# Routing logits from raw rows, a first expert pair selected by products, and filled waits on TensorE, in a two-layer graph and expert network

## The reference

```python
xn = layernorm(x)
x = x + graph_attention(xn, edges) + linear_attention(xn)      # layer 0
x = x + ffn0(layernorm(x))
#   mixed = xn @ wqkv.T ; q, k, v = split(mixed)               # 8 experts
#   logits[e] = sum_j softmax_j(q[e] * k[j]) * v[j]
#   top-2 of logits; scores = softmax(top-2)
#   out = sum over the two experts of score * (silu(a) * g) @ w2[e].T
xn = layernorm(x)
x = x + gat(xn, edges) + (layernorm(linear_attention(xn) @ W_fc + xn) * gamma + beta)
feats = layernorm(x)                                           # layer 1
x = x + ffn1(feats)
#   aff = feats @ centroids.T ; eid = argmax(aff)              # top-1 of 8
#   xhat = layernorm(feats)
#   y = feats + relu((xhat * gamma[e] + beta[e]) @ w1[e] + b1[e]) @ w2[e] + b2[e]
#   out = alpha * y + (1 - alpha) * feats, alpha = sigmoid(aff[eid])
```

## Time and profile before

| | us |
|---|---|
| median of the runs (3) | 1070.32 |
| lowest, highest | 1067.17, 1071.71 |
| the profiled execution | 1067.81 |
| its span, first to last instruction | 1065.9 |

### The profile page before, as it was taken

How to read it: one execution, slowest core, us unless ns; L and a number is a source line. 1 busy time by engine, 2 the same in 40 slices (tenths; PEclk the granted TensorE clock), 3 DMA queues, 4 the chain that set the end, 5 groups by cost and what they waited for, 6 DMA issues and landing times.

```text
span 1065.9 us, 9957 instructions
## 1 busy us (share of the span) xinstructions
PE 1006.1 (94%) x3388; PEld 542.7 (51%) x3388; DVE 362.1 (34%) x1008; ACT 201.7 (19%) x415; POOL 319.5 (30%) x247
## 2 busy tenths in 40 slices
PE   6999999999999999999958999989999999994997
PEld 4555555555555435544445566544444555453332
DVE  6044372156000147701233100171120265576214
ACT  3132321111111038800011111121110020012220
POOL 2888887888888800000000000010000000001210
PEclk9999999999999999999978999999999999995999
DMA  9655545544544630022166898663433115553997
GB/s 334 173 99 145 143 106 140 138 100 90 145 102 99 202 123 2 1 79 79 64 212 197 301 347 325 242 244 100 158 101 110 44 59 208 207 178 121 404 362 258
DMA packets 63852, 174.32 MB, mean 164 GB/s; under 512 B 22224, under 2 KB 22960, under 8 KB 63680
## 3 DMA queue, kind: packets, MB, share of 16 engines
q1 hardware_dynamic: 38800, 146.56, 40.3%
q0 software_dynamic: 20960, 15.63, 8.1%
q10 hardware_dynamic: 4048, 11.59, 3.0%
HBM read 161.79 MB, written 11.95 MB: 163 GB/s over the span
## 4 chain that ended last, share of the span: by engine, by line
PE 46%; POOL 24%; DMA 12%; issue 10%; DVE 6%; ACT 2%; SPq 0%; ACTq 0%; DVEq 0%; POOLq 0%
PE bank L1024 12%; PE bank L1000 10%; POOL n_lo L536 7%; POOL n_hi L536 7%; PE bank L1220 6%; POOL w_lo L536 5%; POOL w_hi L536 4%; PE bank L1013 4%; DMA G<-in_stream 3%; PE bank L1245 2%; PE bank L1112 2%; DMA Y<-in_stream 2%; PE bank L1374 1%; DMA n_hi<-count,ridx 1%; DMA Y<-xs,idx 1%
## 5 line engine op out<-in xcount | busy, mean ns | idle before, releaser
L1013 PE MATMUL bank<-xnT,ring 128*128 128x384 f32 x896 | 291.8, 486 | 1.8 <-ACT xnT L693 1.2
L1013 PEld LDWEIGHTS bank<-xnT,ring 128*128 128x128 f32 x896 | 170.1, 190 | 120.4 <-ACT xnT L693 1.5
L590 POOL DMA_INDIRECT Y<-xs,idx x10 | 10.5, 1046 | 527.6 <-DVE idx L1806 443.4
L536 POOL DMA_INDIRECT n_lo<-count,ridx x48 | 83.2, 1734 | 15.0 <-issue 14.1
L536 POOL DMA_INDIRECT n_hi<-count,ridx x48 | 80.2, 1672 | 16.4 <-issue 14.0
L1024 PE MATMUL bank<-ring,Y 128*128 128x512 f32 x192 | 83.6, 594 | 0.0
L1024 PE MATMUL bank<-ring,xnT 128*128 128x512 f32 x192 | 82.7, 592 | 0.0
L1013 PE MATMUL bank<-Y,ring 128*128 x256 | 82.7, 486 | 0.0
L1220 PE MATMUL bank<-ring,Y 128*128 128x352 f32 x256 | 78.7, 466 | 0.7 <-issue 0.7
L717 ACT ACTIVATE Y<-bank,sbias,scale 128x384 f32 (+1 forms) x48 | 32.2, 671 | 202.3 <-PE bank L1013 184.4
L1000 PE MATMUL bank<-ring,Y 128*128 128x512 f32 x160 | 70.0, 593 | 0.0
(11 more groups left out here) (305 smaller groups left out, 1073.2 us busy)
## 6 DMA issues: line engine op xcount, KB each, us to landing
ring<-in_stream SPq DMA_DIRECT2D x144, 512.0 KB
ring<-in_up SPq DMA_DIRECT2D x32, 704.0 KB, 5.9
Y<-in_stream SPq DMA_DIRECT2D x18, 512.0 KB, 6.6
G<-in_stream SPq DMA_DIRECT2D x16, 512.0 KB, 7.2
ring<-in_dn SPq DMA_DIRECT2D x7, 1024.0 KB, 5.8
rows<-keys SPq DMA_DIRECT2D x10, 512.0 KB
ys<-Y ACTq DMA_DIRECT2D x9, 512.0 KB, 7.6
xnT<-in_stream SPq DMA_DIRECT2D x6, 512.0 KB
```

Of the source, the lines that this page charges most:

```text
L536: pool.indirect_dma_start(table, bass.IndirectOffsetOnAxis(ap=at[:, e:e + 1], axis=0), what[:, e:e + 1], None, **how).then_inc(done, 16)
L590: pool.indirect_dma_start(dst, None, src, bass.IndirectOffsetOnAxis(ap=idx[:, col:col + 1], axis=0))\
L1013: last = pe.matmul(bank[to][:, 0:N], ring[:, r, k * P:(k + 1) * P], rhs(k), start=(k == 0), stop=(k == KB - 1))
```

## The change

1. Attention: `scores(1)` to `scores(4)` stand one behind each of the last four value chunks; `turn` waits for the bank that it writes instead of for all; VectorE weighs unit 2 ahead of reading unit 4.
2. First routing: TensorE transposes halves of the raw rows `xr` as soon as they are in the residual (`turn_raw`). The logits are those of raw rows; VectorE subtracts mean times the column sums of `wqkv` (a product with ones, `gate_sums`) and scales by `rstd` (`route_logits`). Blocks 0 and 1 are routed together, ahead of block 2's addition, block 2 alone. ScalarE takes two exponentials (`GL`, `GM`), with the square root of block 2 between them.
3. Second routing: the residual is written in halves; affinities come from raw rows (`turn_features`, `affinities`), corrected by the mean but not scaled, and the first maximum is taken ahead of the second normalisation. The features `xn` of the last block are written after the routing.
4. The first pair's rows are not gathered: a 0/1 mask `first_pair` is multiplied with the rows `xh` in SBUF (`select_first_pair`), which gives them already transposed. GpSimd gathers pairs 1 to 3 (`pairs`).
5. `keep_busy(n, to)` issues n products of 128x384 f16 into a bank that is not read: 1 + 26 behind the last logits, 3 + 7 in `list_rows`, 4 ahead of and 4 behind the first expert's turn, 6, 10 and 8 in the second routing.
6. `up` and `up_pair` wait for the two halves of the transposed rows apart.

The core of the diff, PE first, then ACT, DVE, POOL and SP:

```diff
+            def keep_busy(n, to):
+                for _ in range(n):
+                    pe.matmul(bank[to][:, 0:N], id16, iota, start=True, stop=True)
...
                 if kk == 0:
                     pe.wait_ge(v2_done, 2)
-                    scores(1)
-                elif kk >= 2:
-                    scores(kk)
-            scores(4)
-            pe.wait_ge(v2_done, 6)
+                scores(kk + 1)
...
+            def turn_raw(half, b):
+
+                pe.wait_ge(x1_done, half * NB + b + 1)
+                pe.wait_ge(t_evicted, T_LN2 + 2 * b + half - 1)
+                for k in range(4):
+                    last = pe.transpose(bank[half][:, k * P:(k + 1) * P],
+                                        xr[:, b, (4 * half + k) * P:(4 * half + k + 1) * P], ident)
+                last.then_inc(tp_ready, 1)
...
+            for b in range(1, NB):
+                block_rows(b, range(0, 2), tok(2), arrived, True, False)
+                for half in range(2):
+                    turn_raw(half, b - 1)
+                if b == 1:
+                    pe.matmul(bank[5][:, 24:48], ones, small_sums, start=True, stop=True).then_inc(pe_output, 1)
+                block_rows(b, range(2, 4), tok(2), arrived, False, False)
+                for half in range(2):
+                    raw_logits(b - 1, half)
                 block_rows(b, gnn_slots, tok(4), arrived, False, True)
-                if b:
-                    if b == 1:
-                        pe.wait_ge(x1_done, NB)
-                    logits(T_LN2, wqkv, 3 * NE, b - 1)
-            turn_block(T_LN2, NB, NB - 1)
-            logits(T_LN2, wqkv, 3 * NE, NB - 1)
+            turn_raw(0, NB - 1)
+            turn_raw(1, NB - 1)
+            raw_logits(NB - 1, 0)
+            keep_busy(1, 6)
+            raw_logits(NB - 1, 1)
+            keep_busy(26, 6)
...
+                keep_busy(3, spare)
                 for e in range(turns):
+                    if e:
+                        keep_busy(1, spare)
...
             rank_rows(R0)
-            list_rows(R0, NE, lambda b, e: slot[:, b, e, :])
+            list_rows(R0, NE, lambda b, e: slot[:, b, e, :], 6)
+            keep_busy(4, 6)
...
                 turn_rows(S, 0, True)
+                keep_busy(4, 6)
                 pe.wait_ge(R.rows_known, 2)
                 up_(0, 0)
...
+            def select_first_pair(half):
+
+                for k in range(4):
+                    for b in range(NB):
+                        last = pe.matmul(bank[pair_banks(0)[half]][:, k * P:(k + 1) * P],
+                                         YN(3)[:, b, (4 * half + k) * P:(4 * half + k + 1) * P], first_pair[:, b, :],
+                                         start=(b == 0), stop=(b == NB - 1))
+                last.then_inc(M1s.xt_ready, 1)
+
+            pe.wait_ge(R1.slots, 1)
+            pe.wait_ge(xh_ready, NB)
+            select_first_pair(0)
+            pe.wait_ge(R1.slots, 2)
+            for i in range(1, PAIRS):
+                for b in range(NB):
+                    last = pe.matmul(bank[4][:, i:i + 1], pair_slots(b, i), token[:, b:b + 1],
+                                     start=(b == 0), stop=(b == NB - 1))
+            last.then_inc(R1.listed, 1)
+            select_first_pair(1)
...
+            for b in range(NB - 1):
+                seed(1 + b, b, b + 1)
                 evict_block(TP0, b)
-
-
+                store_normed(b)
             act.wait_ge(act_input, GL)
-            act.activation(w[:, 200:392], w[:, 200:392], ACT.Exp).then_inc(act_output, 1)
+            act.activation(w[:, 200:328], w[:, 200:328], ACT.Exp).then_inc(act_output, 1)
+            evict_half(TP0, NB - 1, 0)
+            seed(NB, NB - 1, NB)
+            evict_half(TP0, NB - 1, 1)
+            act.wait_ge(act_input, GM)
+            act.activation(w[:, 328:392], w[:, 328:392], ACT.Exp).then_inc(act_output, 1)
+            store_normed(NB - 1)
...
+            for g in range(4):
                 read_scores(g)
                 if g >= 2:
                     weigh(g - 2)
+            weigh(2)
+            read_scores(4)
...
+                v.wait_ge(pe_output, arrived)
+                for b in range(a, z):
+                    raw = bank[2][:, b * 24:(b + 1) * 24] if b < NB - 1 else bank[5][:, 0:24]
+                    last = stt(mixed[:, b], raw, rstd[:, b:b + 1], shift[:, b], ALU.mult, ALU.subtract)
...
                 normalise_block(xn, xr, b, xn_ready)
+                step(ts(shift[:, b, :], gate_sums, mv[:, b, 0:1], rstd[:, b:b + 1], ALU.mult, ALU.mult))
+                if b == 1:
+                    route_logits(0, 2, MIXED)
+                    route_choice(0, 2, GL)
...
+                step(v.tensor_copy(root[:, b:b + 1], rstd[:, b:b + 1]))
+                if b == NB - 1:
+                    first_choice()
                 rstd_from(9 + 3 * b, b, b + 1)
+                step(tt(both[:, b:b + 1], rstd[:, b:b + 1], root[:, b:b + 1], ALU.mult))
+                ts(xh[:, b, :], xr[:, b, :], mv[:, b, 0:1], both[:, b:b + 1], ALU.subtract, ALU.mult).then_inc(xh_ready, 1)
+                if b < NB - 1:
+                    normalise_features(b)
...
+            route_pairs()
+            normalise_features(NB - 1)
+            step(tt(gat, small(120, 24), aff, ALU.mult))
+            step(v.tensor_reduce(small(204, 3), gat3, AX.X, ALU.add))
+            tt(small(24, 3), small(204, 3), root[:], ALU.mult).then_inc(act_input, 1)
+            v_rows_T(0)
             v.wait_ge(act_output, AF)
             scores(R1, [oh1], [m1], HC, hbase)
...
+            def pairs():
+
+                pool.wait_ge(R1.rows_known, 1)
+                pool.wait_ge(xs_stored, 96)
+                for i in range(1, PAIRS):
+                    if i > 2:
+                        pool.wait_ge(M1s.xt_ready, 2 * i - 2)
+                    gather(Xgs[i % 2], xs, i, odd_gathered if i % 2 else M1s.gathered)
...
-            sp.wait_ge(M1s.gathered, 16)
+            sp.wait_ge(M1s.xt_ready, 2)
             sp.wait_ge(odd_gathered, 16)
```

More of the change, by code:

```diff
@@ L1164, in _, with raw_logits @@
+            def raw_logits(b, half):
+                pe.wait_ge(t_evicted, T_LN2 + 2 * b + half + 1)
+                to = bank[2][:, b * 24:(b + 1) * 24] if b < NB - 1 else bank[5][:, 0:24]
+                for k in range(4 * half, 4 * half + 4):
+                    last = pe.matmul(to, xtok(k, b), wqkv[:, k, :], start=(k == 0), stop=(k == KB - 1))
+                if half and b:
+                    last.then_inc(pe_output, 1)
+            gnn_slots = range(4, 8)
             arrived = 16 * (CH_O // 8 + 2)
@@ new lines, in affinities @@
+            def affinities(b, half):
+                pe.wait_ge(t_evicted, T_FE + 2 * b + half + 1)
+                to = bank[2][:, b * NE:(b + 1) * NE] if b < NB - 1 else bank[5][:, 0:NE]
+                for k in range(4 * half, 4 * half + 4):
+                    last = pe.matmul(to, xtok(k, b), cent[:, k, :], start=(k == 0), stop=(k == KB - 1))
+                if half and b:
+                    last.then_inc(pe_output, 1)
+            pe.wait_ge(zf_done, 2)
+            pe.matmul(bank[5][:, NE:2 * NE], ones, cent_sums, start=True, stop=True).then_inc(pe_output, 1)
@@ L1428, in _ @@
+            for half in range(2):
+                turn_features(half, 0)
             fc_block(2, 0)
-            pe.wait_ge(zf_done, 2)
-            logits(T_FE, cent, NE, 0)
+            for half in range(2):
+                affinities(0, half)
             fc_block(2, 1)
-            for b in range(1, NB):
-                turn_block(T_FE, 3 * NB, b)
-                logits(T_FE, cent, NE, b)
+            for half in range(2):
+                turn_features(half, 1)
+            for half in range(2):
+                affinities(1, half)
@@ L1435, in _ @@
+            keep_busy(6, 3)
+            for half in range(2):
+                turn_features(half, 2)
+            for half in range(2):
+                affinities(2, half)
+            keep_busy(10, 7)
             rank_rows(R1)
+            keep_busy(8, 7)
             def pair_slots(b, i):
                 return hslot[:, b, 2 * i:2 * i + 2, :].rearrange("p e n -> p (e n)")
-            list_rows(R1, PAIRS, pair_slots)
-            for n in range(DIRECT):
-                for b in range(NB):
-                    last = pe.matmul(bank[5 + n][:, b * P:(b + 1) * P], pair_slots(b, PAIRS - DIRECT + n), id16,
-                                     start=True, stop=True)
-                last.then_inc(turned_ready, 1)
+            def select_first_pair(half):
+                for k in range(4):
+                    for b in range(NB):
[3 more added lines that the diff above has]
+                last.then_inc(M1s.xt_ready, 1)
@@ L1710, in take_av @@
                     .then_inc(av_taken, 1)
-            for g in range(5):
+            for g in range(4):
                 read_scores(g)
@@ L2096, in _ @@
                 rstd_from(7 + 3 * b, b, b + 1)
```

(10 more changed lines are left out.)

263 lines of the change are left out of this document (156 added, 107 removed).

## The result

| | before | after |
|---|---|---|
| median, us | 1068.74 (4 runs) | 1055.83 (4 runs) |
| lowest, highest | 1066.21, 1071.71 | 1054.85, 1057.97 |
| span of the profiled execution | 1065.9 | 1053.5 |

The ratio is 0.9881, with a 95% interval of 0.9848 to 0.9914: faster by 1.2%. The forecast of 1057.0 is 1.2 us from the median. It was taken from a median before of 1070.3, which is 1068.7 here: a gain of 13.3 us was forecast, and the medians differ by 12.9. The spans of the two profiled executions differ by 12.4 us. One term of the 13.3, however, was wrong by a factor of nearly three, and three others made up for most of it. So I read the places again, each with its own shift between the two traces.

A forecast was written before the change was run, and what follows sets the result against it. TensorE, busy 94% of the span, was taken to bound the kernel outside its gaps, with the tail ending with the weight stream. Gains of 2.8 + 6.5 + 4 = 13.3 from 1070.3 gave 1057.0 us; range 1052 to 1065.

The forecast's parts named there:

- Attention, 2.8: Start of attention: score units moved one chunk forward let ScalarE's copies start earlier; gain 1.9 to 2.9 us, taken as 2.8.
- First routing, 6.5: First routing: raw-row logits and fills bring the first expert earlier; 8.0 us with clock held, 2.9 low, taken as 6.5.
- one-hots 5.0 earlier: First routing, last block: one-hots ready at 552.0 us against 557.01, 5.0 earlier.
- fall and recovery: First routing: the clock falls before the 26 fills and they lift it halfway; the whole part then gains 6.4 us.
- The sign named for the routing of blocks 0 and 1: First routing, VectorE: the forecast would be wrong if this routing delays the last addition; only 0.7 us of cover left.
- The table switch: First routing, ScalarE: switching tables for the square root between two copies costs 1.28 us per switch; 0.4 is lost.
- Second routing, 4: Second routing and tail: raw rows and selection release the weight stream earlier; 4.5 us with clock held, taken as 4.
- gather 2: Tail: gather 2, issued earlier, leaves the full DMA stretch: 0.5 MB at 409 GB/s, 1.3 us.
- Rival 1: Clock stays low through lists, selection and first expert; gain only 5.8 us, 1064.5; chance 0.18.
- Rival 2: Second routing: the weight stream is not released earlier, so that part gives nothing; 1061.0 us; chance 0.14.
- Rival 3: Both routings: slow fills and selection block TensorE's in-order queue, delaying first expert and release; 1072.3 us; chance 0.05.
- all parts held: Whole kernel: gains of 2.9 + 8.0 + 4.5 us and more, below 1053.5; chance 0.05.

## Why the prediction was right, point by point

- **Attention, 2.8: 3.5.** The mechanism was right. I had charged 0.85 for the moved unit. It costs nothing, since it stands in TensorE's queue either way; the wait fell by 2.1 and the 18 turns by 1.4 with the clock held. The experiment with this part alone shows both rows.
- **First routing, 6.5: 2.3.** This is the term that was mis-sized. The step "one-hots 5.0 earlier" held (4.7 beyond the shift of attention), and "routing of one block 4.7" held: 544.12 to 549.03 is 4.9. The step that failed is the silent one behind it, that the gather follows the one-hots at the old distance: the change moves the last block's store behind the exponential, and the prediction did not list it among the instructions of the moved step. The gather started 5.2 us earlier (554.10 for 559.26), of which 3.5 are attention's; of the 4.7, 3.0 were lost to the store. The runs show it: the releaser of the gather's row is the store with and without fills, and becomes the row numbers once the loads beside it are held. Its new place in ScalarE's queue is the smaller part: issued ahead of the exponential it landed 1.45 earlier and still decided. The larger part is its 8 us beside the weight loads, which the kernel before had too, unseen: without them it is 2.8. The second part of the term, the clock, was taken as fall and recovery (1.4 to 3.0 of gain); the expert's products gave 1.0 (10.23 for 11.23), less 0.35 for longer fills. The sign named for the routing of blocks 0 and 1 did not show: VectorE was idle for 1.36 us ahead of the last addition.
- **The table switch.** It was priced at 1.28 from its row, with no drain, and took that: in the chain of waits above, the copy of 0.60 at 540.02 is followed by the load at 540.63 and the square root at 541.93. The page "ScalarE: Activation LUTs" of the Trainium skill (What ACT_TABLE_LOAD costs) adds a drain of about 1.38; between the end of the copy (540.62) and the square root (541.93) there are 1.31 us for load and drain together, so the trace does not agree.
- **Second routing, 4: 5.3.** One-hots 6.2 earlier were 6.3; row numbers 3.1 were 4.0, since the mask stood 0.35 sooner than worked out, 12 products of the selection took 2.94, not 3.1, and the lists behind them 0.24, not 0.7; release 3.2 was 4.3. With the clock held the prediction had 4.5, and it took 4 for the risk that it falls. The full stretch is 1.0 shorter from the release to the end, where I took 1.3 for gather 2; the run that holds gather 2 gives it only 0.4, so the rest has another cause, which stays open.
- **A gain nobody forecast, 1.3.** At the start of layer 1 a wait of 2.02 us for a weight chunk is a wait of 0.74 for a copy. Half of it is that SyncE issued the first chunks 6.6 us earlier (694.78 for 701.42), behind a gather of the last expert's rows, where TensorE's work just ahead came 6.0 earlier. The other half is that the chunk landed sooner behind its issue (5.6 us at most instead of 6.1). Neither was tested.
- **Rival 1** (clock low throughout) was half true: in the first routing the clock was low from 552, in the second it held, and without fills the second routing lost 5.0 us by the medians. The page "TensorE: Matmul & The Clock Gate" of the Trainium skill (Part 4: PE-mode transpose) says that turns do not count as activity as products do. With the fills gone the clock was at 0.50 over 956 to 960, in the affinities behind the last turns, which agrees, though TensorE was idle for 1.75 us just ahead of these turns and no run separates the two. **Rival 2** was wrong: the release came 4.3 earlier. **Rival 3** did not decide the result, but its queue of slow fills stands in three traces, at 544.68 with the loads held, at 544.98 with the lists ahead, and at 956.92 with 14 fills.

The total came out right because +0.7, +1.3 and +1.3 stood against −4.2. That is a matter of luck; the range, from all parts held to all clocks low, was what carried it. The range's lower end was wrongly added up: all parts held, 2.9 + 8.0 + 4.5, is 1054.9 and not below 1053.5.

## What to carry to other kernels

When a chain is shortened by 5 us, list everything that used to be hidden behind it and when each of these ends, not only what stands in the chain: a store of 8 us that starts when the chain starts becomes the chain. Look also at what makes such a transfer long: here it was 8 us beside weight loads that nobody needed yet, and 2.8 us without them. Look for the last instruction ahead of the shortened one on every queue that the next step waits for, and at where the change itself moves that store in its queue. Fills pay where TensorE's next work stands in the chain that ends last, as in the second routing here, and not where that work waits for a transfer anyway, as in the first. A fixed number of them is a bet on the clock, since the same fills take 1.6 to 1.7 times as long once it has fallen, and stand in the way of what comes next.

## What the runs showed that I had not expected

- A store of 512 KB from ScalarE's queue took 8.15 us to land beside 2.8 MB of weight loads issued 4 to 6 us before it (DMA share 0.98 to 1.08 until 551); with those loads held it took 2.8 us.
- Code that these variants leave as it is has its clock held in some traces and not in others. The 26 fills of the first routing took 4.38 us in the changed kernel and 6.97 or 7.00 in two variants; a block's eight turns in the second routing took 1.3 us there and 2.0 in two others. Each variant has one trace, so what decides it is not known. The mean granted clocks of the changed kernel's four runs, 0.990 to 0.995, do not order their times (0.994 for 1054.85 and for 1057.97), so part of the spread has another source, which I did not find.
